# Sums over sources by VectorE additions ahead of the products with ones, and the first in-degrees ahead of a norm's transposes

## The reference

```python
x = layernorm(x + gat(x))      # 2 layers: 8 heads of 768, then 1 head
x = layernorm(x + rgat(x))     # 3 relations; 4 heads of 192, then 1 head
x = layernorm(x + rgcn(x))     # 3 layers, 4 relations
x = layernorm(x + gcn(x))      # 2 layers

# a GAT layer, per head
e = exp(leaky_relu(alpha_s[src] + alpha_d[dst]) - max_over_incoming_edges)
out = segment_sum(h[src] * e / (segment_sum(e, dst)[dst] + 1e-16), dst)

# an RGCN layer
out = x @ root + b
for r in range(4):             # deg: number of incoming edges of type r
    out += segment_sum((x @ W[r])[src] / max(deg_r[dst], 1), dst)
```

## Time and profile before

| | us |
|---|---|
| median of 3 runs | 1827.55 |
| lowest, highest | 1824.73, 1829.87 |
| profiled execution, its own time | 1827.02 |
| its span, first to last instruction | 1825.2 |

### The profile page before, as it was taken

How to read it: one execution, slowest core, us unless ns; L and a number is a source line. 1 busy time by engine, 2 the same in 40 slices (tenths; PEclk the granted TensorE clock), 3 DMA queues, 4 the chain that set the end, 5 groups by cost and what they waited for, 6 DMA issues and landing times. The chain is left out here.

```text
span 1825.2 us, 26385 instructions
## 1 busy us (share of the span) xinstructions
PE 1770.4 (97%) x8951; PEld 1484.9 (81%) x8953; DVE 1175.0 (64%) x2220; ACT 714.0 (39%) x1153; POOL 745.9 (41%) x622
## 2 busy tenths in 40 slices
PE   8999899999999999998999899999999999999998
PEld 3444597999999999877986699987888888899977
DVE  9999676887787877566758946775224222444556
ACT  0112535454454444333466644433224223433131
POOL 1556341523424424211677775522334333433322
PEclk9999999999999999998999999999999999999999
DMA  1000651312312224122320032212222223322231
GB/s 21 1 23 34 243 160 57 105 54 86 96 53 96 80 68 148 52 70 84 110 67 1 1 107 74 97 58 75 66 88 87 75 81 90 91 80 90 87 129 53
DMA packets 54205, 143.22 MB, mean 78 GB/s; under 512 B 13780, under 2 KB 13908, under 8 KB 53076
## 3 DMA queue, kind: packets, MB, share of 16 engines
q1 hardware_dynamic: 47332, 108.48, 19.2%
q10 hardware_dynamic: 6768, 33.30, 5.0%
HBM read 129.18 MB, written 12.58 MB: 78 GB/s over the span
## 5 line engine op out<-in xcount | busy, mean ns | idle before, releaser
L776 POOL TENSOR_TENSOR w_pair<-early,w_pair 128x384 fp32r<-128x384 f32 x468 | 490.8, 1085 | 825.1 <-ACT w_pair L1502 825.1
L861 PE MATMUL ps<-w_pair,cols_x 128*128 128x384 f32 x2088 | 375.3, 336 | 0.6 <-DVE al_part L1922 0.6
L861 PEld LDWEIGHTS ps<-w_pair,cols_x 128*128 128x128 f32 x2088 | 361.9, 188 | 6.2 <-issue 3.6
L861 PE MATMUL ps<-w_pair,wide 128*128 128x384 f32 x1872 | 334.4, 338 | 4.4 <-DVE wide L1913 3.1
L861 PEld LDWEIGHTS ps<-w_pair,wide 128*128 128x128 f32 x1872 | 328.4, 190 | 9.7 <-DVE wide L1913 5.0
L1502 ACT ACTIVATE w_pair<-early 128x768 fp32r<-128x768 f32 x234 | 181.7, 840 | 315.0 <-PE ps L861 147.8
L1437 PE MATMUL ps<-wide,w_pair 128*128 128x512 f32 x972 | 226.5, 391 | 2.7 <-DVE wide L1913 2.7
L1437 PEld LDWEIGHTS ps<-wide,w_pair 128*128 128x128 f32 x972 | 181.1, 188 | 42.1 <-DVE wide L1913 5.2
L436 PE MATMUL count_ps<-early,src_hot 128*128 (+1 forms) x814 | 179.8, 383 | 7.8 <-DVE early L356 7.6
L436 PEld LDWEIGHTS count_ps<-early,src_hot 128*128 (+1 forms) x816 | 80.4, 99 | 106.8 <-issue 10.2
L356 DVE TENSOR_SCALAR early<-node_f,edge_f,weight 128x512 f16 x204 | 147.9, 775 | 0.0
(11 more groups left out here) (273 smaller groups left out, 2386.7 us busy)
## 6 DMA issues: line engine op xcount, KB each, us to landing
early<-weights SPq DMA_DIRECT2D x240, 384.0 KB, 3.1
edge_mask<-counts ACTq DMA_DIRECT2D x13, 512.0 KB, 3.2
multi<-attn ACTq DMA_DIRECT2D x8, 768.0 KB, 4.8
kept<-early ACTq DMA_DIRECT2D x3, 1536.0 KB, 6.1
counts<-out SPq DMA_DIRECT2D x7, 512.0 KB, 2.6
multi<-kept ACTq DMA_DIRECT2D x2, 1536.0 KB, 7.6
edge_mask<-masks ACTq DMA_DIRECT2D x5, 512.0 KB, 3.5
last_raw<-weights SPq DMA_DIRECT2D x6, 384.0 KB, 6.3
```

Source lines behind the costliest of these rows:

```text
L776: return nc.gpsimd.tensor_tensor(dst, whole, high.bitcast(F32), ALU.subtract)
L861: mm = nc.tensor.matmul(ps[:, m, 0:HW], left[:, a, k, m * P:(m + 1) * P], w_pair[:, slot_of[0], b, k, :], start=(k == 0 and a + b == 0), s ...
```

## The change

The sums over sources are taken in two steps. VectorE first adds the four blocks of a matrix elementwise; PE then multiplies the one sum with ones.

In the eight heads the sum of the blocks before rounding goes to `prob_sum`, which is the memory of `hv`; three additions, one in each of the slots s = 2, 3, 4. ScalarE makes its high part in `den_pair` (the memory of `xt`) after the high part of block 3, VectorE the low part after the low part of block 3, and PE does two matmuls in place of eight. Since `hv` is taken, the row tiles of all heads go directly: one copy by ScalarE, low part and dots of VectorE from PSUM, and PE waits for `rows_ready` in place of `tile_copied` before it writes the bank again.

For the in-degrees VectorE adds the four blocks of the integer counts into `r_den` in fp32 (`count_sum`), and PE multiplies it in full fp32 (no split): one matmul in place of eight, and for the last degrees four with two columns in place of 32. ScalarE may load new counts only once the sum is made. The sum and the matmul for relation 0 move: the sum ahead of the second norm on VectorE, the matmul ahead of that norm's transposes on PE, into bank 3.

The diff, cut to its core:

```diff
@@ in graph_layers
+        with nc.sbuf_tensor("den_pair", [P, 2, N], F32R) as den_pair:
+            pass
         xt = sb("xt", [P, 2, N], F32)
+        prob_sum = hv_rows[:, 0:N]
@@ PE, head
-                            product(j_rows, m, cols_x, rows_ready if h < 2 else tile_copied, h * 8 + (4 + m + 1))
+                            product(j_rows, m, cols_x, rows_ready, h * 8 + (4 + m + 1))
                         else:
-                            product(j_rows + 1, m, cols_x, tile_copied if with_last else rows_ready, h * 8 + (8 + m + 1))
+                            product(j_rows + 1, m, cols_x, rows_ready, h * 8 + (8 + m + 1))
...
                 pe.wait_ge(vb_ready, h + 1)
-                for s in range(NB):
-                    for a in range(2):
-                        mm = nc.tensor.matmul(ps[:, 6, :], ones[:], prob[:, a, s, :], start=(s + a == 0), stop=(s + a == NB))
+                pe.wait_ge(den_lo, h + 1)
+                for a in range(2):
+                    mm = nc.tensor.matmul(ps[:, 6, :], ones[:], den_pair[:, a, :], start=(a == 0), stop=(a == 1))
@@ PE, out_product
-                        product(j, m, cols_y[0], tile_copied, x_head * 8 + (16 + 4 + m + 1))
+                        product(j, m, cols_y[0], rows_ready, x_head * 8 + (16 + 4 + m + 1))
@@ PE, degrees
-            def degrees(spread_only):
-                for s in range(NB):
-                    for a in range(2):
-                        mm = nc.tensor.matmul(ps[:, 5 if spread_only else 6, :], ones[:], prob[:, a, s, :], start=(s + a == 0), stop=(s + a == NB))
+            def degrees(i, spread_only, bank=5):
+                pe.wait_ge(deg_sum, 3 * (i + 1))
+                mm = nc.tensor.matmul(ps[:, bank if spread_only else 6, :], ones[:].bitcast(F32), r_den[:], start=True, stop=True)
                 if not spread_only:
                     for m in range(NB):
-                        for s in range(NB):
-                            for a in range(2):
-                                mm = nc.tensor.matmul(ps[:, 7, 2 * m:2 * m + 2], prob[:, a, s, m * P:(m + 1) * P], ones[:, 0:2],
-                                                      start=(s + a == 0), stop=(s + a == NB))
+                        mm = nc.tensor.matmul(ps[:, 7, 2 * m:2 * m + 2], r_den[:, m * P:(m + 1) * P], ones[:, 0:2].bitcast(F32),
+                                              start=True, stop=True)
...
             pe.wait_ge(den_read, 4)
+            degrees(0, True, LAST_BANK[6])
             turn(KB * 2, ready=NB)

             def next_degrees(r):
-                pe.wait_ge(cnt_lo, r + 2)
                 pe.wait_ge(y_done, KB * (r + 1))
-                degrees(True)
-
-            def first_degrees():
-                pe.wait_ge(cnt_lo, 1)
-                degrees(True)
+                degrees(r + 1, True)
...
-            column_product(44, cols_x, True, False, KB * 2, meanwhile={2: first_degrees, 3: first_sums, 4: lambda: next_degrees(0)})
+            column_product(44, cols_x, True, False, KB * 2, meanwhile={2: lambda: pe.wait_ge(deg_read, 1), 3: first_sums, 4: lambda: next_degrees(0)})
@@ ScalarE
-                        copy_tile(j_rows + n, m, n, h * 8 + (8 + u), rows[1 - parity], direct=not with_last)
+                        copy_tile(j_rows + n, m, n, h * 8 + (8 + u), rows[1 - parity], direct=True)
...
+                    if s == NB:
+                        act.wait_ge(den_sum, 3 * h + 3)
+                        copy(den_pair[:, 0], prob_sum).then_inc(den_hi, 1)
...
             def load_count(number, matrix):
                 act.wait_ge(cnt_lo, number)
+                if number <= REL4:
+                    act.wait_ge(deg_sum, 3 * number)
@@ VectorE, rows_tile
-                           [(vec[:, v], al[:, parity, v]) for v in range(2)], direct=x_head < 2)
+                           [(vec[:, v], al[:, parity, v]) for v in range(2)], direct=True)
@@ VectorE, prob_slot
                 if 1 <= s <= NB:
+                    if s >= 3 and h < HEADS0:
+                        dve.wait_ge(den_sum, 3 * h + (s - 2))
                     weigh(...)
                 if s >= 2:
                     low(...)
+                if 2 <= s <= NB and h < HEADS0:
+                    dve.wait_ge(x_mid, h * 10 + s)
+                    if s > 2:
+                        dve.wait_ge(den_sum, 3 * h + (s - 2))
+                    add(prob_sum, y_tiles[0] if s == 2 else prob_sum, y_tiles[(s - 1) % 2]).then_inc(den_sum, 1)
+                if s == NB + 1 and h < HEADS0:
+                    dve.wait_ge(den_hi, h + 1)
+                    sub(den_pair[:, 1], prob_sum, f32(den_pair[:, 0])).then_inc(den_lo, 1)
@@ VectorE, RGCN
+            def count_sum(i):
+                add(r_den[:], cnt16[:, 0, :], cnt16[:, 1, :]).then_inc(deg_sum, 1)
+                for s in range(2, NB):
+                    dve.wait_ge(deg_sum, 3 * i + s - 1)
+                    add(r_den[:], r_den[:], cnt16[:, s, :]).then_inc(deg_sum, 1)
...
+            dve.wait_ge(cnt_in, 16 * 5)
+            count_sum(0)
             block_norm(1, relation_rows, order=BLOCK_ORDER)
...
-                        nc.vector.transpose(scale_bc[:, r], ps[:, 5, :]).then_inc(deg_read, 1)
+                        nc.vector.transpose(scale_bc[:, r], ps[:, 5 if r else LAST_BANK[6], :]).then_inc(deg_read, 1)
...
                         count_low(number + 2)
+                        if number + 1 < REL4:
+                            count_sum(number + 1)
...
                         count_low(13)
+                        dve.wait_ge(diag_added, 1)
+                        count_sum(REL4)
```

More of the change, by code:

```diff
@@ L664, in graph_layers @@
         vb_ready = sem("vb_ready")
+        den_sum = sem("den_sum")
+        den_hi = sem("den_hi")
+        den_lo = sem("den_lo")
+        deg_sum = sem("deg_sum")
         u_done = sem("u_done")
@@ L1486, in _ @@
             pe.wait_ge(scale_ready, REL4)
-            degrees(False)
+            degrees(REL4, False)
             layer_product(72, cols_y[1], added)
```

## The result

The changed kernel takes 1818.4 us (median of 5 runs, 1818.12 to 1824.4) against 1827.94 us of before in the same comparison: ratio 0.9946, 95% interval 0.9922 to 0.9971. That is 9.5 us, against a forecast of 9.1. The profiled execution is the slowest of the five, 1824.4 us with a span of 1822.6; its trace shows most of the gain, and why this one execution has only 2.6 us of it. One execution of a later version (both mended) took 2907 us and one of the kernel before beside the last version 3548 us; the ratios leave these two out.

The account below looks back on a forecast made before the run. The prediction took PE, busy 97% of the span, as the bound. Its terms summed to -9.1 us against the profiled 1827.02, hence 1817.9, rounded to 1818; 8-in-10 range 1811.5 to 1824, leaving out the slower bank-release rival.

Parts of the forecast that it names:

- Heads 1 to 6: Steady heads: six of eight denominator matmuls leave PE, no stall taken; 8.4 us gained, at worst 4.8.
- last degrees: Final in-degrees: 3.3 us gained (2.3 to 3.9) by fewer matmuls, 1.6 more (0 to 1.6) without the clock fall behind.
- The tiles' copies: Row tiles in the steady heads: one ScalarE copy saved, bank released by VectorE's dots; nothing, up to 0.3 us a head.
- Head 0: PE already waits here: VectorE and ScalarE delay shows whole, +2.2 us (1.4 to 3.4); one clock fall, +1.6 (0 to 1.7).
- Head 7: Final GAT head: chain of 3.6 us against 3.1 free, 0.4 of waiting; 1.0 us gained (0 to 1.4).
- First degrees: Relation 0's degrees: matmuls -1.87, later second norm +1.5, fp32 matmul in PE's gap +0.3; sum -0.1 us (-1.7 to +0.9).
- Relation 1: Its degrees: additions lengthen PE's wait to 3.6 us, net +1.3 (1.0 to 1.5); clock fall +1.6 (0 to 1.7).
- (a): Rival: the clock doesn't fall in the two longer gaps, at head 0 and relation 1; 1814.7 us, chance 0.2.
- (b): Rival: VectorE contention makes all new operations long, 0.6 us waiting per steady head, 0.4 more in head 7; 1821.9, chance 0.12.
- (c): Rival: last degrees keep their clock fall and the small fp32 matmuls cost their upper bound; 1820.5 us, chance 0.1.
- (e): Rival: a degree's fp32 matmul costs as much as eight of the others; 1821.4 us, chance 0.07.
- (d): Rival: late bank release makes PE stand at product 7 of heads 0 to 6, 2.2 us each; 1833.4 us, chance 0.06.

Follow-up runs that it names:

- both mended: Changed kernel with head 0 keeping eight matmuls, relation 1's sum ahead of relation 0's edge tiles, ScalarE's first weight split for relation 1 earlier: 1813.67 us, ratio 0.9915.

## Why the prediction was right, point by point

The forecast of 1818.0 met the median of 1818.4, and the main mechanisms were those named: matmuls taken off PE where it was the bound, idle time with a low clock behind it where it was not. That the number came so close is luck: the heads gave 3.1 us where the terms say 5.6, the degrees 7.1 where they say 3.5, and the two misses cancelled.

- *Heads 1 to 6, last degrees.* Right to a tenth of a microsecond in sum, -8.40 and -4.64: behind the last degrees the clock stays at 1.00. Within the second, two sizes were off and cancelled: the degrees gave 3.69 for 3.3, the product behind them 0.95 for 1.3. Its first eighteen matmuls are 1.5 us faster by the clock (3.24 for 4.78), but PE then waits 0.28 us for VectorE in its middle and loses some 0.3 more around it.
- *The tiles' copies.* Right: nothing, by an experiment of its own.
- *Head 0.* The delay was right (2.25 for 2.2). The step of the sum that was mis-sized is the price of the clock: 1.6 was taken from the fall behind the last degrees, and it is 3.2 to 4.1. Here two gaps followed one another, and the low level lasted some ten us, through the small matmuls and the first half of the aggregation. I had priced a fall as one amount; its length differs by place (3.4 us at 0.50 behind the last degrees of the kernel before, 10.2 here).
- *Head 7.* -1.0 was wrong in sign, +0.35. The chain was sized at 3.6 us against 3.1 free, and it is 4.65. It is 1.50 for the last addition, 1.48 for the subtraction and the longer operations around them, all beside 12 us of GpSimd, and PE waits 1.54. The bound of 5.2 for "all long" was the nearer end here, as the early operations of head 7 lie before GpSimd starts and the late ones all beside it.
- *First degrees.* -0.1 became -1.9. The norm's first tile was delayed by 0.8, its transposes by 0.9, not 1.5: the counts had landed, one addition took 0.69 and the two beside GpSimd 2.12 together, not 3.0. The matmul cost nothing instead of 0.3; in the four of the other kernels in which it met the low clock it did delay the fourth transpose by 0.3. And with the matmul in the gap the low clock was 3.4 us long instead of 6.8, worth 1.0, which I had left out.
- *Relation 1.* The wait was 3.66 as forecast (3.6), +1.1 net. The clock's fall was forecast as certain and came in four of seven. ScalarE's late weight splits, which I called hidden, are a wait of 1.31 us in the fifth edge tile (0.36 before) and took most of relation 2's gain. For the three relations together the sum said +1.2 (1.3 + 1.6 - 1.7); it is 0.0.
- *Rivals.* (a), no falls, is refuted at head 0 and half true at relation 1. (b), contention with a wait in each steady head, is refuted there and true in head 7. (c) and (e) are refuted: full clock behind the last degrees, four small fp32 products in 0.81 us, 0.86 us for a large one. (d) is refuted by the kernel with direct tiles alone.
- *What I didn't see.* +0.65 us at the end: PE waits 1.32 instead of 1.04 and 0.78 instead of 0.43 us in the GCN. The longer first wait (1.31 to 1.37) stands in all kernels with the change of the degrees, 1.04 in the three without, so some of the gain is given back there.

## What to carry to other kernels

Moving a sum from PE to VectorE pays where PE is the bound and costs its whole chain where PE already waits, so decide it place by place: here head 0 on the old way was worth more than half of the heads' steady gain. A wait on PE is to be priced with the clock behind it, and matmuls placed in the wait, even ones whose result nobody reads, held the clock at both places where they were tried. A slack read behind work at low clock is smaller at full clock, as in head 7. When a wait is removed, look at once for the engine that stands next in line: relation 1's wait of 3.66 us came back as 3.08 us in the fifth edge tile, and with ScalarE's order changed 1.66 us of it was still there.

## What the runs showed of the hardware

- The low clock lasted 3.4 us behind some gaps, 6.8 or ten behind others. After equal waits of 3.65 us it fell in four executions of seven, after 1.08 to 1.10 us in two of six; where the gap was filled with matmuls it stayed at 1.00, in one profiled execution at each of two places.
- VectorE's operation with two SBUF inputs (128x512) took 0.69 us alone and 1.50 beside GpSimd, and was short again when GpSimd had ended (three in 3.65 us).
- A full fp32 matmul appears as two records, of which the start-to-start distance to the next matmul shows only half the price (0.45 of 0.86 us); the rest appears in the block behind, 4.69 for 4.24 us. Four more of them cost 3.44 us.
- The same 300 us of instructions took 302.0 to 309.1 us in the fourteen profiled executions.
